# Second attention of a fused decoder: steps of two heads by one query block, spread inverse sums, output weight in the last pair

## The chip, the cores and the metric

One core of one Trainium2 chip runs the whole kernel. The metric is the device time in microseconds of one execution; lower is better. TensorE (PE) multiplies matrices into PSUM banks of 512 f32 columns, VectorE (DVE) and ScalarE (ACT) read PSUM, GpSimd (POOL) works on SBUF alone, and SyncE (SP) issues the transfers. Each engine takes its instructions in order and waits on semaphores.

## The reference

Two decoder layers on x of 2 x 512 tokens by 128: gated linear attention, cross attention, a mixture of experts; then a T5 attention, a bidirectional attention with a context and a quantized feed-forward layer. The change touches the T5 attention ("the second attention") alone. With 16 heads of 64 it computes, on normalised x:

```python
q, k, v = x @ wq, x @ wk, x @ wv                 # 128 -> 16 heads x 64, each
s = q @ k.T + bias[head, bucket(key - query)]    # no scale; bias from rel_bias
p = softmax(s)
x = x + concat_heads(p @ v) @ wo                 # 1024 -> 128
```

## The kernel before

A row is one head by one block of 128 queries: 16 heads x 2 batches x 4 blocks = 128 rows. Heads come in eight pairs (`PAIRS`); a pair has `ROWS` = 16 rows, two pairs make one turn of a loop (`BODY` = 32), and all engines run `t5_steps`: step s issues row s's scores and later stages of earlier rows (`on(s, lag, last)`), so that a row is drawn out over `LAG` = 8 steps. The order within a step is written out by hand on each engine.

Per row. TensorE: scores (L1220, f16 operands split in a high and a low part; the split halves of q lie one above the other in the 128 rows, 2 products of 512 columns) into bank 0 or 1; four transposes of the exponentials (L854) into bank 2 or 3; the context (L1231, 8 f16 products of 128 columns, probabilities split in two) into bank 4; the product with the head's rows of the output weight (L1211, f32, two passes) into bank 5. VectorE: scores plus bias strip, with the row minimum of the negated sum (L1707, `SN`, `nmx`); the reciprocal of the sum (L1690); the low part of the probabilities (L1720). ScalarE: exponential with row sum (L797); the high part of the probabilities (L810); eviction of the context (L791, `CTT`); eviction of the output product scaled by the inverse sum (L785, `OS`). POOL adds `OS` to X (L531), copies the bias strips and splits the qkv weights.

The projections of the next pair are 12 jobs (`t5_job`), one in each of 12 of the 16 steps: three or six products into bank 6 or 7 (L1184 for q and k, L1180 for v), the high part by ScalarE (`high_part`, L771, L769), the low part by VectorE (`low_part`, L1683). SyncE then lays the parts of q and k one above the other by eight transfers per pair (`stack_pair`, L356, L360), and loads the pair's rows of the output weight twice. For pair 0 these jobs and transfers come ahead of step 0.

After the last row, `norm_stats` and `norm_rows` of the first four tiles run inside the last steps (`NORM_STEP`), then the next attention begins (L1735).

## Time and profile before

| | us |
|---|---|
| median of 3 runs | 546.7 (546.38 to 551.78) |
| profiled execution | 549.21 |
| its span, first to last instruction | 547.4 |

The page gives busy time by engine. A timeline line gives the start and length of an instruction or of a few merged ones; engines start an instruction before the one ahead has left the pipe, so the distance from start to start is what one costs in a stream, and the length is what a waiter sees. The TensorE clock is given as a share of 2.4 GHz.

### The profile page before, as it was taken

What the parts mean: (1) busy time and instruction counts of PE and PEld (TensorE: products, weight loads), DVE (VectorE), ACT (ScalarE), POOL (GpSimd) and SP (SyncE); (2) the same over time, 40 slices, a digit from 0 to 9 for tenths busy, and PEclk for the clock granted to TensorE, in tenths of its full rate; (3) what the DMA queues carried; (4) which work ended last, traced back from release to release, by engine and by line L of the source; (5) the groups of instructions that cost most, each with busy time, mean ns of one, the idle gap of its engine ahead of it and who ended that gap; (6) DMA issues with size and microseconds to landing.
All of it is one profiled execution on the core that took longest, in us unless ns stands there. A gap on an engine that the chain in (4) does not pass through costs nothing.

```text
span 547.4 us, 12975 instructions
## 1 busy us (share of the span) xinstructions
PE 481.9 (88%) x4074; PEld 373.9 (68%) x4074; DVE 410.5 (75%) x1154; ACT 363.6 (66%) x996; POOL 159.6 (29%) x292
## 2 busy tenths in 40 slices
PE   4699858998786998549999989999999999989997
PEld 1245545777672776427888878887888888867866
DVE  3856858676776799738889878887898898754675
ACT  3834434444328587329999999998999999932140
POOL 4091352000013357201343324332433322230100
PEclk9989989999987899679999999999999999996899
DMA  7499553000000020061414140412423230000001
GB/s 235 65 102 104 65 176 123 1 1 1 2 0 10 30 72 25 1 131 38 95 39 104 27 106 11 97 43 50 91 49 77 49 79 1 2 2 1 0 1 40
DMA packets 23839, 29.32 MB, mean 54 GB/s; under 512 B 2262, under 2 KB 14848, under 8 KB 23789
## 3 DMA queue, kind: packets, MB, share of 16 engines
q1 hardware_dynamic: 23789, 28.73, 24.9%
q8 instruction: 22, 0.36, 0.3%
q14 instruction: 28, 0.23, 0.1%
HBM read 11.42 MB, written 4.72 MB: 29 GB/s over the span
## 4 chain that ended last, share of the span: by engine, by line
PE 52%; ACT 18%; DVE 16%; issue 9%; POOL 2%; DMA 1%; ACTq 0%; SPq 0%; POOLq 0%; DVEq 0%
PE bank L854 8%; ACT PT L810 8%; PE bank L1220 5%; PE bank L1231 5%; PE bank L1211 4%; PE bank L1078 4%; ACT PEX L797 4%; PE bank L1148 3%; PE bank L1135 3%; PE bank L859 2%; PE bank L1030 2%; ACT OS L785 2%; POOL X L531 2%; PE bank L1184 2%; DVE Y L1360 2%
## 5 line engine op out<-in xcount | busy, mean ns | idle before, releaser
L531 POOL TENSOR_TENSOR X<-X,OS 128x128 f32<-128x128 f32 x128 | 58.4, 456 | 179.9 <-ACT OS L785 179.9
L797 ACT ACTIVATE PEX<-SN,nmx 128x512 f32<-128x512 f32 x128 | 100.2, 782 | 9.4 <-DVE nmx L1707 9.4
L1707 DVE CUSTOM_DVE_ANT_0 SN<-bank,strip 128x512 f32<-128x512 f32 x128 | 86.4, 675 | 8.8 <-PE bank L1220 8.7
L1720 DVE TENSOR_TENSOR PT<-bank,PT 128x512 f16<-128x512 f32 x128 | 87.4, 683 | 1.5 <-ACT PT L810 1.3
L1231 PEld LDWEIGHTS bank<-PT,TV 128*128 128x128 f16 x1024 | 67.8, 98 | 29.0
L1220 PE MATMUL bank<-TK,TQ 128*128 128x512 f16 x256 | 77.3, 385 | 7.9 <-DMA TK<-RAWK 7.9
L810 ACT CAST PT<-bank 128x512 f16<-128x512 f32 x128 | 82.4, 643 | 0.3 <-PE bank L854 0.3
L1231 PE MATMUL bank<-PT,TV 128*128 128x128 f16 x1024 | 78.1, 219 | 0.0
L854 PE MATMUL bank<-cs,PEX 128*128 128x128 f32 x512 | 77.8, 275 | 0.2 <-DVE PT L1720 0.2
L785 ACT ACTIVATE OS<-bank,rps 128x128 f32<-128x128 f32 x128 | 56.0, 438 | 4.8 <-issue 3.6
L854 PEld LDWEIGHTS bank<-cs,PEX 128*128 128x128 f32 x512 | 57.0, 142 | 1.3 <-issue 0.4
L1211 PE MATMUL bank<-wos,CTT 128*128 128x128 f32 x256 | 53.2, 290 | 4.4 <-ACT OS L785 3.4
L1211 PEld LDWEIGHTS bank<-wos,CTT 128*128 128x128 f32 x256 | 38.4, 189 | 9.1 <-issue 3.3
L1690 DVE RECIPROCAL rps<-psm 128x1 f32<-128x1 f32 x128 | 20.9, 163 | 30.1 <-PE bank L1220 29.6
L791 ACT COPY CTT<-bank 128x128 f32<-128x128 f32 x128 | 41.0, 320 | 0.5 <-PE bank L1231 0.3
L1184 PE MATMUL bank<-YP,WP 128*128 128x256 f16 x192 | 33.1, 293 | 1.5 <-DVE YP L1671 1.4
L859 PE MATMUL bank<-ones 128*128 128x128 f32 x244 | 33.1, 292 | 0.0
L1220 PEld LDWEIGHTS bank<-TK,TQ 128*128 128x128 f16 x256 | 25.2, 99 | 11.0 <-issue 8.6
L859 PEld LDWEIGHTS bank<-ones 128*128 128x128 f32 x244 | 30.9, 205 | 1.6 <-issue 1.6
L797 ACT ACTIVATION_READ_ACCUMULATOR PEX<-SN,nmx 128x1 f32 x128 | 31.6, 247 | 0.0
L1613 DVE TENSOR_TENSOR HID<-PT,HID 128x512 f16<-128x512 f32 x32 | 25.8, 846 | 5.7 <-ACT HID L742 5.1
L1148 PE MATMUL bank<-w2p,HID 128*128 128x128 f16 x384 | 24.4, 227 | 6.2 <-DVEq L1636 3.7
(279 smaller groups left out, 912.9 us busy)
## 6 DMA issues: line engine op xcount, KB each, us to landing
TK<-RAWK SPq DMA_DIRECT2D x32, 256.0 KB, 4.4
bias_rows<-biasr SPq DMA_DIRECT2D x1, 4096.0 KB, 43.5
TQ<-RAWQ SPq DMA_DIRECT2D x32, 128.0 KB, 2.4
band<-bias_rows SPq DMA_DIRECT2D x1, 3072.0 KB, 11.5
wqkv<-in_twqkv SPq DMA_DIRECT2D x8, 192.0 KB, 3.9
w1s<-in_w SPq DMA_DIRECT2D x8, 128.0 KB, 2.1
w2s<-in_w SPq DMA_DIRECT2D x8, 128.0 KB, 2.1
wos<-in_two SPq DMA_DIRECT2D x16, 64.0 KB, 2.3
```

Source lines behind the costliest of these rows:

```text
L531: gp.tensor_tensor(x_tile, x_tile, OS[:, r % 2, :], ALU.add).then_inc(sm["to_ready"], 1)
L785: sc.activation(OS[:, r % 2, :], bank[5][:, 0:P], ACT.Copy, scale=rps[:, r % 8:r % 8 + 1]).then_inc(sm["os_ready"], 1)
L797: sc.activation(PE_[:, r % 2, :], SN[:, r % 2, :], ACT.Exp, bias=nmx[:, r % 2:r % 2 + 1], scale=-1.0, accum_out=psm[:, r % 8:r % 8 + 1]).t ...
L810: sc.copy(PT1[:, r % 4, :], bank[2 + r % 2][:, :]).then_inc(sm["pt1_ready"], 1)
L854: return nc.tensor.transpose(out_, in_, ident[0:n, 0:n])
L859: mm(bank[b][:, 2 * P:3 * P], ones[:, :], ones[:, :], start=True, stop=True)
L1184: ins = mm(o[:, 0:2 * P], WP[u][:, w_part, w:w + P], YP[:, x_part, 2 * P * g:2 * P * g + 2 * P], start=(k == 0), stop=(k == 2))
L1211: mm(bank[5][:, 0:P], CTT[:, r % 2, :], wos[u][:, h, :], start=True, stop=True).then_inc(sm["to_mm"], 1)
L1220: ins = mm(bank[s % 2][:, :], TQ[u][:, h, S * b + P * qt:S * b + P * qt + P], TK[u][:, part, h, S * b:S * b + S], start=(part == 0), stop= ...
L1231: ins = mm(bank[4][:, 0:P], TV[u][:, TG * b + kt, h, :, :].rearrange("p n d -> p (n d)"), pt[:, r % 4, P * kt:P * kt + P], start=(part == ...
L1707: vv.tensor_tensor_reduce(out=SN[:, r % 2, :], in0=bank[r % 2][:, :], in1=strip[u][:, h, c:c + S], scale=-1.0, scalar=3.0e38, op0=ALU.add, ...
L1720: vv.tensor_tensor(PT2[:, r % 4, :], bank[2 + r % 2][:, :], PT1[:, r % 4, :], ALU.subtract).then_inc(sm["pt2_ready"], 1)
```

## The change

A step is now two heads by one query block: 64 steps, `ROWS` = 8 and `BODY` = 16 for a turn of two pairs, lag 5. The heads of a pair sit in rows 0 to 63 and 64 to 127 of q and k as the projection leaves them: the stacking transfers and the raw copies are gone, and the scores are three products (high x high, high x low, low x high) of 64 rows for each head, alternating between the heads. Exponentials overwrite `SN`, a ring of four. The transposed probabilities are f32 (head 0 evicted by ScalarE, head 1 by VectorE), v stays f32, and the context of both heads goes to the two column halves of bank 6. The inverse sums are spread over 64 partitions per head by a product with the identity (columns 128 to 255 of bank 6), copied to `rpb` by ScalarE, and VectorE multiplies the context by them while it evicts it to `CTX`, which keeps all pairs. The product with the output weight (loaded once, whole, to `WO`) is issued in the last pair alone: in each of its eight steps seven products for one tile of X, and from step 13 to 20 of the last turn one more with the last pair's context; VectorE adds each result to X. Projections are six jobs of 512 columns, all through bank 7; the v jobs have no low part. Those of pair 0 use four banks, and its v jobs come behind the scores of step 0. The core of the diff:

```diff
 TH, TD = 16, 64
 PAIRS = TH // 2
-ROWS = 2 * NT
+ROWS = NT
 BODY = 2 * ROWS
-LAG = 8
-NORM_STEP = BODY + 3
-PROJECTIONS = [(kind, g) for kind in "qkv" for g in range(NT // 2)]
+LAG = 5
+RING = 4
+NORM_STEP = BODY + 2
+PROJECTIONS = [("q", 0), ("k", 0), ("q", 1), ("k", 1), ("v", 0), ("v", 1)]
 JOBS = len(PROJECTIONS)
-JOB_BANKS = (6, 7, 4, 5)
-JOBS_FROM = 2
-STACK = 8 * 16
+SPLIT_JOBS = 4
+JOB_BANK = 7
+FIRST_BANKS = (6, 7, 4, 5, 6, 7)
+JOBS_FROM = 1
...
-            RAWQ = t5("RAWQ", [P, 2, TOK], F16)
-            RAWK = t5("RAWK", [P, 2, TOK], F16)
             TQ = [t5(f"TQ{u}", [P, 2, TOK], F16) for u in range(2)]
-            TK = [t5(f"TK{u}", [P, 2, 2, TOK], F16) for u in range(2)]
-            TV = [t5(f"TV{u}", [P, NT, 2, 2, TD], F16) for u in range(2)]
-            SN = t5("SN", [P, 2, 512])
-            nmx = t5("nmx", [P, 2])
-            PE_ = t5("PEX", [P, 2, 512])
-            psm = t5("psm", [P, 8])
-            rps = t5("rps", [P, 8])
-            PT1 = t5("PT1", [P, 4, 512], F16)
-            PT2 = t5("PT2", [P, 4, 512], F16)
-            CTT = t5("CTT", [P, 2, P])
-            OS = t5("OS", [P, 2, P])
+            TK = [t5(f"TK{u}", [P, 2, TOK], F16) for u in range(2)]
+            TV = [t5(f"TV{u}", [P, NT, P]) for u in range(2)]
+            SN = t5("SN", [P, RING, 2, S])
+            nmx = t5("nmx", [P, RING, 2])
+            psm = t5("psm", [P, RING, 2])
+            rps = t5("rps", [P, RING, 2])
+            PTO = t5("PTO", [P, 2, S])
+            PTE = Z[:, :, :].rearrange("p (h t) c -> p h (t c)", h=2)
+            CTX = t5("CTX", [P, PAIRS, TOK])
+            rpb = YT[:, 0:P]
+            WO = XB
+            def probs_t(r, h):
+                return (PTE, PTO)[r % 2][:, h, :]
...
+            sp.wait_ge(sm["x_done"], 4)
+            sp.dma_start(WO[:, :, :], two.rearrange("(n p) c -> p n c", p=P)).then_inc(sm["ld_wo"], 16)
+            for pair in range(PAIRS):
+                if pair >= 2:
+                    sp.wait_ge(sm["tw_split"], (pair - 1) * 2)
+                pair_qkv(pair, pair % 2)
...
-                if on(s, LAG, last):
-
-                    r = s - LAG
-                    u, b, qt, h = where(r)
-                    pool.wait_ge(sm["os_ready"], n - 7)
-                    pool.wait_ge(sm["to_ready"], n - 6)
-                    x_tile = X[:, TG * b + qt, :]
-                    gp.tensor_tensor(x_tile, x_tile, OS[:, r % 2, :], ALU.add).then_inc(sm["to_ready"], 1)
...
+                if on(s, 1, last):
+                    r = s - 1
+                    for h in range(2):
+                        act.wait_ge(sm["ttr_ready"], (n - 1) * 2 + h + 1)
+                        p = SN[:, r % RING, h, :]
+                        sc.activation(p, p, ACT.Exp, bias=nmx[:, r % RING, h:h + 1], scale=-1.0,
+                                      accum_out=psm[:, r % RING, h:h + 1]).then_inc(sm["exp_ready"], 1)
+                if on(s, 4, last):
+                    act.wait_ge(sm["tpv_mm"], n - 3)
+                    if s >= 5:
+                        act.wait_ge(sm["ctt_ready"], n - 4)
+                    sc.copy(rpb[:, :], bank[6][:, P:2 * P]).then_inc(sm["rb_ready"], 1)
                 if on(s, 2, last):
-                    act.wait_ge(sm["ttr_ready"], n - 1)
                     r = s - 2
                     if s >= 4:
-                        act.wait_ge(sm["tt_mm"], n - 3)
-                    sc.activation(PE_[:, r % 2, :], SN[:, r % 2, :], ACT.Exp, bias=nmx[:, r % 2:r % 2 + 1], scale=-1.0,
-                                  accum_out=psm[:, r % 8:r % 8 + 1]).then_inc(sm["exp_ready"], 1)
-                job = t5_job(s - 1, last)
+                        act.wait_ge(sm["tpv_mm"], n - 3)
+                    act.wait_ge(sm["tt_mm"], (n - 2) * 2 + 1)
+                    sc.copy(probs_t(r, 0), bank[4][:, :]).then_inc(sm["pta_ready"], 1)
+                job = t5_job(s, last)
                 if job:
                     j, u, ahead = job
-                    if j == 0:
-
-                        act.wait_ge(sm[f"stack{1 - u}"], (i + ahead + u) * STACK)
-                    high_part(((i + ahead) * 2 + u) * JOBS, j, u)
-                if on(s, 3, last):
-
-                    r = s - 3
-                    act.wait_ge(sm["tt_mm"], n - 2)
-                    sc.copy(PT1[:, r % 4, :], bank[2 + r % 2][:, :]).then_inc(sm["pt1_ready"], 1)
-                if last and s == NORM_STEP + 2:
+                    high_part(i * 2 + ahead, j, u)
+                if last and s == NORM_STEP + 1:
...
+            def out_tile(tile, pairs, done):
+                pe.wait_ge(sm["ctt_ready"], pairs[-1] * ROWS + tile + 1)
+                pe.wait_ge(sm["to_ready"], done)
+                for p in pairs:
+                    ins = mm(bank[JOB_BANK][:, 0:P], CTX[:, p, P * tile:P * tile + P], WO[:, p, :], start=(p == pairs[0]), stop=(p == pairs[-1]))
+                ins.then_inc(sm["wo_mm"], 1)
             pe.wait_ge(sm["tw_split"], 2)
-            for j in range(JOBS):
-                if j >= 4:
-                    pe.wait_ge(sm["pj_ready"], j - 3)
-                project(0, j, 0, 4)
-            pe.wait_ge(sm["pj_ready"], JOBS)
+            for j in range(SPLIT_JOBS):
...
+                    u, b, qt = where(s)
+                    if qt == 0:
+                        pe.wait_ge(sm["pj_ready"], (i * 2 + s // ROWS) * SPLIT_JOBS + 2 * b + 2)
                     if s >= 2:
-                        pe.wait_ge(sm["ttr_ready"], n - 1)
-                    for part in range(2):
-                        ins = mm(bank[s % 2][:, :], TQ[u][:, h, S * b + P * qt:S * b + P * qt + P],
-                                 TK[u][:, part, h, S * b:S * b + S], start=(part == 0), stop=(part == 1))
-                    ins.then_inc(sm["ts_mm"], 1)
-                if on(s, 5, last):
-                    r = s - 5
-                    u, b, qt, h = where(r)
-                    if s >= 6:
-                        pe.wait_ge(sm["ctt_ready"], n - 5)
-                    for part, (pt, ready) in enumerate(((PT1, "pt1_ready"), (PT2, "pt2_ready"))):
-                        pe.wait_ge(sm[ready], n - 4)
-                        for kt in range(TG):
-                            ins = mm(bank[4][:, 0:P], TV[u][:, TG * b + kt, h, :, :].rearrange("p n d -> p (n d)"),
-                                     pt[:, r % 4, P * kt:P * kt + P], start=(part == 0 and kt == 0), stop=(part == 1 and kt == TG - 1))
-                    ins.then_inc(sm["tpv_mm"], 1)
+                        pe.wait_ge(sm["ttr_ready"], (n - 1) * 2)
+                    pe.wait_ge(sm["ln_yt"], 10)
+                    for k, (q_part, k_part) in enumerate(PRODUCTS):
+                        for h in range(2):
+                            r = slice(TD * h, TD * h + TD)
+                            ins = mm(bank[2 * (s % 2) + h][:, :], TQ[u][r, q_part, S * b + P * qt:S * b + P * qt + P],
+                                     TK[u][r, k_part, S * b:S * b + S], start=(k == 0), stop=(k == 2))
+                            if k == 2:
+                                ins.then_inc(sm["ts_mm"], 1)
+                    if s == 0:
+                        for j in range(SPLIT_JOBS, JOBS):
+                            pe.wait_ge(sm["pj_ready"], j - SPLIT_JOBS + 1)
+                            project(j, 0, FIRST_BANKS[j])
...
+                if on(s, 2, last):
+                    r = s - 2
+                    if s == 2:
+                        pe.wait_ge(sm["pj_ready"], SPLIT_JOBS)
+                    for h in range(2):
+                        pe.wait_ge(sm["exp_ready"], (n - 2) * 2 + h + 1)
+                        if s >= 3:
+                            pe.wait_ge(sm[("pta_ready", "ptb_ready")[h]], n - 2)
+                        for kt in range(TG):
+                            ins = tr(bank[4 + h][:, P * kt:P * kt + P], SN[:, r % RING, h, P * kt:P * kt + P])
+                        ins.then_inc(sm["tt_mm"], 1)
+                if on(s, 3, last):
+                    r = s - 3
+                    u, b, qt = where(r)
+                    if qt == 0:
+                        pe.wait_ge(sm["pj_hi"], (i * 2 + r // ROWS) * JOBS + SPLIT_JOBS + b + 1)
+                    if s >= 4:
+                        pe.wait_ge(sm["ctt_ready"], n - 3)
+                    pe.wait_ge(sm["rps_ready"], n - 2)
+                    for h in range(2):
+                        mm(bank[6][TD * h:TD * h + TD, P:2 * P], rps[:, r % RING, h:h + 1].to_broadcast([P, TD]), ident, start=True, stop=True)
+                    pe.wait_ge(sm["pta_ready"], n - 2)
+                    pe.wait_ge(sm["ptb_ready"], n - 2)
+                    for kt in range(TG):
+                        for h in range(2):
+                            d = slice(TD * h, TD * h + TD)
+                            ins = mm(bank[6][d, 0:P], TV[u][:, TG * b + kt, d], probs_t(r, h)[:, P * kt:P * kt + P],
+                                     start=(kt == 0), stop=(kt == TG - 1))
+                    ins.then_inc(sm["tpv_mm"], 1)
+                for done, tile, pairs in out_tiles(s, last):
+                    if done == 0:
+                        pe.wait_ge(sm["ld_wo"], 16)
+                        pe.wait_ge(sm["pj_hi"], PAIRS * JOBS)
+                    out_tile(tile, pairs, done)
...
+                    if (s - 1) % ROWS == 0:
+                        dve.wait_ge(sm["strip_ready"], (i * 2 + (s - 1) // ROWS + 1) * 6)
+                    if s >= 5:
+                        dve.wait_ge(sm["tt_mm"], (n - 4) * 2)
+                    dve.wait_ge(sm["ts_mm"], n * 2)
+                    dve.sem_inc(sm["ttr_turn"], 1)
+                for h in range(2):
+                    if on(s, 1, last):
+                        r = s - 1
+                        u, b, qt = where(r)
+                        c = P * (TG - 1 - qt)
+                        vv.tensor_tensor_reduce(out=SN[:, r % RING, h, :], in0=bank[2 * (r % 2) + h][:, :], in1=strip[u][:, h, c:c + S], scale=-1.0,
+                                                scalar=3.0e38, op0=ALU.add, op1=ALU.min,
+                                                accum_out=nmx[:, r % RING, h:h + 1]).then_inc(sm["ttr_ready"], 1)
+                    if h == 0 and on(s, 2, last):
+                        r = s - 2
+                        dve.wait_ge(sm["exp_ready"], (n - 1) * 2)
+                        vv.reciprocal(rps[:, r % RING, :], psm[:, r % RING, :]).then_inc(sm["rps_ready"], 1)
+                if on(s, 4, last):
+                    r = s - 4
+                    u, b, qt = where(r)
+                    dve.wait_ge(sm["rb_ready"], n - 3)
+                    c = P * (TG * b + qt)
+                    dst = CTX[:, bass.ds(i * 2 + r // ROWS, 1), c:c + P].rearrange("p o c -> p (o c)")
+                    vv.tensor_tensor(dst, bank[6][:, 0:P], rpb[:, :], ALU.mult).then_inc(sm["ctt_ready"], 1)
+                if on(s, 2, last):
+                    r = s - 2
+                    if s >= 4:
+                        dve.wait_ge(sm["tpv_mm"], n - 3)
+                    dve.wait_ge(sm["tt_mm"], (n - 1) * 2)
+                    vv.tensor_copy(probs_t(r, 1), bank[5][:, :]).then_inc(sm["ptb_ready"], 1)
+                job = t5_job(s, last)
                 if job:
                     j, u, ahead = job
-                    low_part(((i + ahead) * 2 + u) * JOBS, j, u)
-                if on(s, 4, last):
-
-                    r = s - 4
-                    if s >= 8:
-                        dve.wait_ge(sm["tpv_mm"], n - 7)
-                    dve.wait_ge(sm["pt1_ready"], n - 3)
-                    vv.tensor_tensor(PT2[:, r % 4, :], bank[2 + r % 2][:, :], PT1[:, r % 4, :], ALU.subtract).then_inc(sm["pt2_ready"], 1)
+                    if j < SPLIT_JOBS:
+                        low_part(i * 2 + ahead, j, u)
+                for done, tile, pairs in out_tiles(s, last):
+                    dve.wait_ge(sm["wo_mm"], done + 1)
+                    dve.wait_ge(sm["to_ready"], done)
+                    vv.tensor_tensor(X[:, tile, :], bank[JOB_BANK][:, 0:P], X[:, tile, :], ALU.add).then_inc(sm["to_ready"], 1)
 
                 if last and s == NORM_STEP:
-                    dve.wait_ge(sm["to_ready"], n - NORM_STEP + BODY - ROWS // 2 + 2)
+                    dve.wait_ge(sm["to_ready"], 12)
                     norm_stats(6, 0, X)
-                if last and s == NORM_STEP + 3:
+                if last and s == NORM_STEP + 2:
...
+    j, ahead = s % ROWS - JOBS_FROM, s // ROWS + 1
+    if 0 <= j < JOBS and not (last and ahead > 1):
+        return j, ahead % 2, ahead
     return None
+def out_tiles(s, last):
+    order = [(s_, tile, pairs) for s_ in range(ROWS, BODY + LAG)
+             for tile, pairs in ((s_ - ROWS, range(PAIRS - 1)), (s_ - ROWS - LAG, range(PAIRS - 1, PAIRS))) if 0 <= tile < NT]
+    return [(done, tile, pairs) for done, (s_, tile, pairs) in enumerate(order) if s_ == s and last]
```

## Rows read from the trace of the kernel before

**Rows 1.** The page, part 1: busy time, share of the span and instructions by engine.
```profile
PE 481.9 (88%) x4074; PEld 373.9 (68%) x4074; DVE 410.5 (75%) x1154; ACT 363.6 (66%) x996; POOL 159.6 (29%) x292
```
**Rows 2.** Stretches: busy us (x instructions) by engine, TensorE clock, DMA share, GB/s.
```profile
421.00:450.00 29.00, 28.98 (x306) 24.49 (x304) 25.89 (x76) 29.00 (x93) 9.55 (x22) 1.00 0.27 60
450.00:484.00 34.00, 32.62 (x322) 26.46 (x321) 26.82 (x83) 32.12 (x100) 10.54 (x24) 1.00 0.01 2
```
**Rows 3.** Timeline, TensorE, start of the second attention: start, us, instructions, idle before.
```profile
229.07 5.25 PE L1184 MATMUL bank<-YP,WP 128*128 128x256 f16 x24 [1.40 <-DVE YP L1671]
...
243.62 1.86 PE L1220 MATMUL bank<-TK,TQ 128*128 128x512 f16 x4 [7.87 <-DMA TK<-RAWK]
```
**Rows 4.** Timeline, all engines, end of the second attention.
```profile
482.03 1.35 DVE L1360 TENSOR_SCALAR Y<-X,mv,rstd 128x128 f32<-128x128 f32 x4 [1.21 <-ACT rstd L577]
...
483.34 0.46 POOL L531 TENSOR_TENSOR X<-X,OS 128x128 f32<-128x128 f32 x1 [0.55 <-ACT OS L785]
```
**Rows 5.** Timeline, TensorE, one row with a projection.
```profile
311.76 0.49 PE L1184 MATMUL bank<-YP,WP 128*128 128x256 f16 x3
312.09 0.60 PE L854 MATMUL bank<-cs,PEX 128*128 128x128 f32 x4
312.52 0.39 PE L1211 MATMUL bank<-wos,CTT 128*128 128x128 f32 x2
312.75 0.59 PE L1220 MATMUL bank<-TK,TQ 128*128 128x512 f16 x2
313.18 0.61 PE L1231 MATMUL bank<-PT,TV 128*128 128x128 f16 x8
313.63 0.49 PE L1184 MATMUL bank<-YP,WP 128*128 128x256 f16 x3
```
**Rows 6.** Timeline, ScalarE, one row without a projection.
```profile
450.72 0.73 ACT L797 ACTIVATE PEX<-SN,nmx 128x512 f32<-128x512 f32 x1
...
451.44 0.57 ACT L810 CAST PT<-bank 128x512 f16<-128x512 f32 x1
451.90 0.38 ACT L785 ACTIVATE OS<-bank,rps 128x128 f32<-128x128 f32 x1
452.19 0.27 ACT L791 COPY CTT<-bank 128x128 f32<-128x128 f32 x1
452.35 0.72 ACT L797 ACTIVATE PEX<-SN,nmx 128x512 f32<-128x512 f32 x1
```
**Rows 7.** Timeline, VectorE.
```profile
249.56 0.68 DVE L1720 TENSOR_TENSOR PT<-bank,PT 128x512 f16<-128x512 f32 x1
...
250.23 0.67 DVE L1707 CUSTOM_DVE_ANT_0 SN<-bank,strip 128x512 f32<-128x512 f32 x1
250.83 0.08 DVE L1707 DVE_READ_ACCUMULATOR2_ANT nmx<- 128x1 f32 x1
```
**Rows 8.** Timelines of the GLA stage (the first up to 38.30): rows*columns of a product.
```profile
38.15 0.44 PE L922 MATMUL bank<-QX,KC 128*64 128x256 f32 x2
...
38.73 1.10 PE L949 MATMUL bank<-V,AM 128*128 128x64 f32 x8
...
40.35 0.70 PE L938 MATMUL bank<-V,KPT 64*128 64x256 f32 x4
...
40.98 0.70 PE L963 MATMUL bank<-wA,YT 128*128 128x512 f32 x1
```
**Rows 9.** Group of one line: shapes, count, busy us, mean ns, idle before.
```profile
L1492 DVE TENSOR_TENSOR CX<-bank,rc 128x128 f32<-128x128 f32 x8 | 2.3, 291 | 0.5 <-DVE rc L1489 0.2
```
**Rows 10.** Timeline, first row: VectorE's minimum pass, ScalarE's exponential.
```profile
244.79 0.69 DVE L1707 CUSTOM_DVE_ANT_0 SN<-bank,strip 128x512 f32<-128x512 f32 x1 [8.18 <-PE bank L1220]
...
245.53 0.72 ACT L797 ACTIVATE PEX<-SN,nmx 128x512 f32<-128x512 f32 x1 [9.37 <-DVE nmx L1707]
```
**Rows 11.** Timeline, TensorE, at a turn of the loop.
```profile
316.15 0.49 PE L1211 MATMUL bank<-wos,CTT 128*128 128x128 f32 x2 [1.60 <-ACT OS L785]
```
**Rows 12.** Timeline, POOL: one part of a weight split.
```profile
331.48 0.92 POOL L516 TENSOR_TENSOR WP<-wqkv,WP 128x384 f16<-128x384 f32 x1
```

158 lines of the change are left out of this document (34 added, 124 removed).

## The prediction

> **What bounds the kernel now.** I read the page first: TensorE is the busiest engine [rows 1]. The busy time of stretches comes next: between 421 and 450 us TensorE and ScalarE are both busy for practically the whole stretch, at full clock, and VectorE for nine tenths [rows 2]. That is the second attention, the only stage touched. It starts with the first score product at 243.62 us and ends with the last POOL addition, at 483.80 [rows 3, 4]: 240.2 us for 128 rows (one head, one query block), about 1.88 us each.
>
> Three timelines of single rows say why no engine alone can be relieved. On TensorE, start to start, a row costs 0.33 (projection), 0.43 (four transposes), 0.23 (output product, f32, two passes of about 0.11), 0.43 (two 512-column f16 score products of 0.216) and 0.45 us (eight context products of 0.056): 1.87, with no gap [rows 5]. On ScalarE a row without a projection costs 0.72 (exponential with its sum), 0.46 (512-column eviction), 0.29 and 0.16 (the two 128-column evictions): 1.63 [rows 6], and 0.25 more with one. On VectorE it is 0.60 for the minimum pass, 0.67 for the 512-column subtraction with the reciprocal [rows 7]. So TensorE and ScalarE tie at 1.87 in a row with a projection, and ScalarE sets 1.62 without one. One head pair (12 rows with, 4 without) takes about 12 x 1.87 + 4 x 1.62 = 28.9 us.
>
> **The change, per step (two heads, one query block).** TensorE:
> - Scores: six products of 64 rows instead of four of 128. The heads lie in different row halves. Do halves run side by side? The GLA stage has such pairs. Two column halves at line 922 had both started within 0.15 us, and four passes of 256 columns were over 0.58 us after the first; row halves at line 938 took 0.63 [rows 8]. One after another, four such passes would be 4 x 0.22 = 0.88 by the 0.11 of a 128-column pass. So they run in pairs. Scores: 3 x 0.216 = 0.65 (serial: 1.30).
> - Transposes stay: 8 x 0.11 = 0.87.
> - Context in f32, column halves: 16 passes in pairs, 8 x 0.11 = 0.87 (serial 1.75). The spread of inverse sums: 2 x 0.11 = 0.22 more.
> - Projection: the same columns in half as many jobs, 0.65 each, in six of eight steps.
> - Output product: two of 0.23 fewer per step, but see the last pair.
> - Form changes. 0.58 and 0.63 us against 2 x 0.213 leave 0.15 and 0.20 us per group for entering and leaving a tiled form [rows 8]. There are three changes of form per step (row halves, full, column halves): 0.2 + 0.2 + 0.15 = 0.55. I take the whole; zero is the low end, since before has them at 0 in this stage.
>
> TensorE sum: 0.65 + 0.87 + 0.87 + 0.22 + 0.55 = 3.17, with a projection 3.82, against 3.74 and 3.24 for two rows before. The Trainium skill (TensorEngine Tiling (Array Packing), Key Properties) says that changing the tiling mode drains the engine. The trace agrees: line 949 starts 0.58 us behind the start of the group before it, where the streaming alone explains 0.43. By the rule the sum is the one above; without it, it would be 0.55 lower.
>
> ScalarE: 2 x 0.72, one copy of spread sums 0.15 to 0.29, one probability eviction 0.46, a 512-column projection eviction 0.46: 2.65 at most. VectorE: 2 x 0.60, reciprocal and eviction 0.67 together, product at context eviction about 0.2 (length 0.29 for such a shape [rows 9]), low part 0.60: 2.7. Both are relieved, from 3.74. If sums of work decided, TensorE would set the pace.
>
> **But the order of waits decides.** Row s-3's context product may not start before VectorE has evicted row s-4 from bank 6. That eviction waits for the ScalarE copy of spread sums, which is queued behind both exponentials of row s-1; these wait for the minimum passes of the same step. From the start of the first minimum pass: 0.74 to the first exponential (244.79 to 245.53, [rows 10]), +0.72 second exponential at 1.46, +0.72 copy at 2.18, ready at 2.50 (0.32; the like eviction has a length of 0.27 [rows 6], and I add 0.05 for the handover), VectorE product 2.52 to 2.81, TensorE starts at 2.85.
>
> Loop A, in steps with a q or k projection: behind the copy (2.18) ScalarE evicts the probabilities (+0.16), then the projection (+0.46), which takes 0.60 till VectorE can begin the low part (the like cast has a length of 0.57 [rows 6]), which holds VectorE for 0.60, before the next step's minimum pass: 2.18 + 0.16 + 0.46 + 0.60 + 0.60 = 4.0, with waits between 4.05. A v projection has no low part now, so TensorE's own 3.82 decides. With none: 2.81 less the overlap = 2.78, +0.60 for the VectorE eviction = 3.4. A pair: 4 x 4.05 + 2 x 3.82 + 2 x 3.4 = 30.6 us, against 28.9. So the middle loses 1.7 us per pair although every engine but TensorE has less to do.
>
> **The last pair.** Each of steps 56 to 63 issues seven f32 output products, 14 passes x 0.11 = 1.54 us. Total output work falls (64 instead of 128 products), but where it sits matters: VectorE's addition from bank 7 is the last thing in its step, and its next minimum pass is queued behind it. The loop is 2.85 (to the context product) + 0.15 + 0.22 + 0.87 (spread and context) + 0.2 (change of form) + 1.54 + 0.3 (end of product to VectorE) = 6.1, +0.2 for the addition's issue distance: about 6.2 us per step. Steps 61 to 63 have a second product and addition, serial through the same bank: +0.75. Last pair: 5 x 6.2 + 3 x 6.95 = 51.9 us, where before spent 16 x 1.62 = 25.9. POOL's additions, hidden before (they run 0.46 us after the row's last eviction, and nobody waits for them but POOL [rows 4]), move into this loop. The product of the first step also waits for the output weight and the last projection, both long done. The drain: step 64 has the loop to the context and one short product, 2.85 + 1.24 + 0.8 = 4.9; the two last contexts go copy, VectorE product, spread, context, output product, addition one after another, 0.3 + 0.3 + 1.24 + 0.8 = 2.6 each; two short products 0.8 each; and on VectorE's queue the normalised rows of four tiles, 1.35 [rows 4], and their statistics, put at 0.9: about 14.
>
> **The start.** The eight stacking DMAs per pair and SyncE's waits for them vanish; only the first is exposed, as TensorE's 7.87 us wait [rows 3]. Now four 512-column projections (half the clock there: 24 products of 256 columns took 5.25 us, so 12 of 512 take about 5.1) end at 234.2, the score product follows, the two v projections after it, and their ScalarE evictions (queued ahead of the first exponential) let that begin at 237.4. The first step counts from 236.6. SyncE now loads the whole output weight once, long before, and eight qkv weights; POOL's weight splits (0.92 us for one part [rows 12]) and strip copies (now two in a step) stay off the path: each has two or more steps of slack, no other engine's queue stands behind them but the jobs and minimum passes of the next pairs, and POOL's 128 additions are gone. If that cover went, a split of 1.8 us would show per pair.
>
> **Sum.** Step 1 at 236.6; 55 steps: 7 x 30.6 - 3.4 = 210.8; -1.5 for unfilled first steps; +3.4 for loop turns (one cost TensorE 1.60 us [rows 11], another about as much, the same loop count remains); start of the last pair 449.3; +51.9 = 501.2; +14 = 515.2. Before: 483.8. Difference +31.4. The profiled execution took 549.2 us (span 547.4), so about 580.6; the median of the three runs is 546.7, 2.5 lower: **578 us**.
>
> **Rivals.**
> - R1, only TensorE's work counts (queues run ahead, waits hide): a pair is 6 x 3.82 + 2 x 3.17 = 29.3, a last-pair step 3.17 + 1.54 = 4.7. Ends at 236.6 + 201.9 - 1.5 + 3.4 + 37.7 + 10 = 488, +4: 551; within 1%. For it: ring buffers of four; against: bank 6 and bank 7 are single. Chance 0.08. A mixture, loop A real but last pair shorter (5 us a step), gives 568 and belongs to the forecast.
> - R2, the other side: changes of form cost nothing when products queue up, and the copy is never late. The pace is then 3.17 - 0.55 = 2.62, and 3.27 with a projection, 24.9 a pair, 4.2 a last-pair step: 236.6 + 171.7 - 1.5 + 3.4 + 33.6 + 10 = 454, so 517, faster. It decides once form changes and waits together cost under 0.5 us per step. For it: all three engines' sums are below before's. Against: [rows 8] and loop A, made of instructions each priced. Chance 0.12.
> - R3, halves don't overlap at N = 128 and here (serial): +0.65 + 0.87 + 0.22 = 1.74 per step: 4.9 and 5.55 a step, 43.2 a pair, last-pair steps 7.3: 578 + 7 x 12.6 + 9 = about 675. Against: [rows 8]. Chance 0.05. Partly (weight loads not hidden in a half, +0.4 a step): about 600, in the range.
> - R4, the clock falls: TensorE is busy 4.7 of 6.2 us in the last pair. Before, the clock stays at 2.4 GHz between 450 and 484 [rows 2] with less work at the end. Chance 0.03, +15 us.
>
> **Numbers.** Forecast 0.72, R1 0.08, R2 0.12, R3 0.05, R4 0.03. About 1% is what a measurement can tell from no change. Faster by over 1%: 0.12 (R2). Within 1%: 0.08. Slower: 0.80. Unknown terms: forms 0.55 down to 0.3 (only v and empty steps move, -5 us), copy and handover latencies 0.1 a step (7 us), last pair 5.3 to 7 us a step (-7, +6), unhidden weight loads (+20). With R1 inside, the range is 550 to 602; the forecast's own part of it is 560 to 602.
>
> **What would show it.** Loads at the score product: alternate heads start a few ns apart. Minimum passes two by two, with pairs of steps 4.0 to 4.1 us apart in four of eight, 3.8 in two, 3.4 in two; TensorE idle ahead of the spread product, released by VectorE's context eviction; steps of about 6.2 us in the last eight, the minimum pass waiting behind the addition; the first score product near 234.4; last addition near 514. Wrong if steps of the middle come under 3.6 us on average, or the last pair under 40 us.

## The result, and the profile after

The changed kernel took 581.2 us (median of 4 runs, 579.2 to 584.3), the kernel before 549.2 us beside it (median of 4, 546.4 to 557.6): 1.060 times as long, with a 95% interval from 1.051 to 1.070. (Ratios, here and below, are of fast executions alone; one that took over 1.5% more than the fastest of its kernel, such as the one of 557.6, is left out.) The forecast was 578, in a range from 550 to 602. The profiled execution took 581.8 us with a span of 580.0, against a span of 547.4 before.

The page and its groups of instructions (columns: count, busy us, mean ns, idle before and what ended it), after:

```profile
PE 490.6 (85%) x4234; PEld 351.0 (61%) x4234; DVE 368.7 (64%) x1042; ACT 291.6 (50%) x692; POOL 103.9 (18%) x164
...
L738 ACT ACTIVATE SN<-SN,nmx 128x512 f32<-128x512 f32 x128 | 91.4, 714 | 99.0 <-DVE nmx L1664 99.0
...
L1677 DVE TENSOR_TENSOR CTX<-bank,YT 128x128 f32 (+1 forms) x64 | 18.6, 291 | 70.6 <-ACT YT L744 70.6
```

ScalarE idles 99.0 us ahead of its exponentials, always for VectorE's minimum, and VectorE idles 70.6 us ahead of the context eviction, always for ScalarE's copy of the spread sums (YT is the memory in which that copy lies). The engines now wait for one another in a ring. The windows of [rows 2] have changed in the same way; the middle of the stage and the last pair, after:

```profile
421.00:448.40 27.40, 25.46 (x282) 17.76 (x284) 18.48 (x54) 18.19 (x48) 0.91 (x3) 1.00 0.00 1
454.56:496.00 41.44, 31.48 (x306) 24.14 (x300) 17.00 (x57) 14.81 (x42) 0.00 (x0) 1.00 0.00 1
```

The columns after the length are PE, PEld, DVE, ACT and POOL with their instructions, then the granted clock. Before, TensorE and ScalarE filled their stretch. Now ScalarE is busy for two thirds of the first one and for a third of the second, and even TensorE leaves 10 of 41 us free in the last pair. The clock is full in both, so it explains nothing here.

**A step of the middle** (q or k projection), first minimum pass at 302.80, next one at 306.80. VectorE:

```profile
302.80 0.68 DVE L1664 CUSTOM_DVE_ANT_0 SN<-bank,strip 128x512 f32<-128x512 f32 x1
...
305.34 0.29 DVE L1677 TENSOR_TENSOR CTX<-bank,YT 128x128 f32 x1 [1.18 <-ACT YT L744]
305.55 0.68 DVE L1683 COPY Z<-bank 128x512 f32<-128x512 f32 x1
306.19 0.69 DVE L1646 TENSOR_TENSOR TK<-bank,TK 128x512 f16<-128x512 f32 x1
306.80 0.68 DVE L1664 CUSTOM_DVE_ANT_0 SN<-bank,strip 128x512 f32<-128x512 f32 x1
```

ScalarE and TensorE in the same step:

```profile
303.52 0.72 ACT L738 ACTIVATE SN<-SN,nmx 128x512 f32<-128x512 f32 x1 [1.36 <-DVE nmx L1664]
304.24 0.71 ACT L738 ACTIVATE SN<-SN,nmx 128x512 f32<-128x512 f32 x1
304.95 0.24 ACT L744 COPY YT<-bank 128x128 f32<-128x128 f32 x1
305.10 0.58 ACT L750 COPY Z<-bank 128x512 f32<-128x512 f32 x1
305.57 0.59 ACT L726 CAST TK<-bank 128x512 f16<-128x512 f32 x1
```
```profile
303.36 0.82 PE L1128 MATMUL bank<-YP,WP 128*128 128x512 f16 x3
304.02 1.04 PE L798 MATMUL bank<-cs,SN 128*128 128x128 f32 x8
305.69 0.44 PE L1196 MATMUL bank<-cs,rps 128*64 128x128 f32 x4 [0.63 <-DVE CTX L1677]
305.95 1.04 PE L1202 MATMUL bank<-PTO,TV 128*64 128x128 f32 x16
306.93 0.39 PE L1155 MATMUL bank<-TK,TQ 64*128 64x512 f16 x2
```

Read as a loop: minimum 302.80, first exponential 303.52, second 304.24, copy 304.95, probabilities 305.10, cast 305.57, low part 306.19, next minimum 306.80. That is 4.00 us, and TensorE stands idle for 0.63 of them, released by the context eviction.

**A step of the last pair**, first minimum pass at 454.56, next one at 460.65:

```profile
454.56 0.69 DVE L1664 CUSTOM_DVE_ANT_0 SN<-bank,strip 128x512 f32<-128x512 f32 x1
...
456.71 0.24 ACT L744 COPY YT<-bank 128x128 f32<-128x128 f32 x1
...
456.99 0.29 DVE L1677 TENSOR_TENSOR CTX<-bank,YT 128x128 f32<-128x128 f32 x1 [1.06 <-ACT YT L744]
...
457.34 0.44 PE L1196 MATMUL bank<-cs,rps 128*64 128x128 f32 x4 [1.30 <-DVE CTX L1677]
457.61 1.04 PE L1202 MATMUL bank<-Z,TV 128*64 128x128 f32 x16
458.58 1.83 PE L1136 MATMUL bank<-XB,CTX 128*128 128x128 f32 x14
460.34 0.82 PE L1155 MATMUL bank<-TK,TQ 64*128 64x512 f16 x6
460.44 0.29 DVE L1692 TENSOR_TENSOR X<-bank,X 128x128 f32<-128x128 f32 x1 [2.56 <-PE bank L1136]
460.65 0.68 DVE L1664 CUSTOM_DVE_ANT_0 SN<-bank,strip 128x512 f32<-128x512 f32 x1
```

VectorE waits 2.56 us for the fourteen output passes, and the next minimum pass is queued behind the addition. (XB is the memory in which the whole output weight lies.)

The start and the end of the stage, after (compare [rows 3] and [rows 4]):

```profile
231.54 4.95 PE L1128 MATMUL bank<-YP,WP 128*128 128x512 f16 x12 [1.40 <-DVE YP L1639]
...
236.43 0.82 PE L1155 MATMUL bank<-TK,TQ 64*128 64x512 f16 x6
...
237.76 0.68 DVE L1664 CUSTOM_DVE_ANT_0 SN<-bank,strip 128x512 f32<-128x512 f32 x1
```
```profile
512.33 0.29 DVE L1692 TENSOR_TENSOR X<-bank,X 128x128 f32<-128x128 f32 x1 [0.64 <-PE bank L1136]
512.53 3.04 DVE L1328 TENSOR_SCALAR Y<-X,mv,rstd 128x128 f32<-128x128 f32 x4
515.50 0.54 DVE L1707 TENSOR_SCALAR RH<-wB,colp 128x77 f32<-128x77 f32 x2
```

**Where the 32.6 us went** (580.0 less 547.4). From the first projection to the end of the stage it was 254.7 us before (229.07 to 483.80) and is 284.0 now (231.54 to 515.50): +29.2. The stages ahead, with the same code, ran 2.5 us later in this execution; what follows took 64.5 instead of 63.6. Within the 29.2, cut at the minimum passes of the same rows in both traces: the start gave 9.5 back (from the first projection to the first minimum pass 6.2 instead of 15.7, most of it the score product, 4.89 behind the first projection instead of 14.55). The middle cost 8.6 more (210.7 against 202.1), the last pair 25.9 more (52.0 against 26.1), and the drain behind it 4.2 more (15.1 against 10.9).

The middle lost less than the 7 x 1.7 of the prediction, for two reasons. A pair without a turn of the loop had taken 29.1 us in the trace before and not 28.9, so that the loss per pair is 1.5. And the two turns of the loop had cost 2.1 and 1.7 us before (pairs of 31.2 and 30.8), and cost 0.5 and 0.2 after. The unfilled first steps took a part of this back: they shorten the first pair by 0.8 us, and did by 2.1 before.

### The profile page after: what moved, and what is told of

Its sections match the earlier page's. It is cut to its first block, busy times and chain, and to the rows that moved or that the text cites. A ratio compares the mean times of both kernels' runs of the same rounds, so it can differ in the third digit from the quotient of the medians.

```text
span 580.0 us, 12093 instructions
## 1 busy us (share of the span) xinstructions
PE 490.6 (85%) x4234; PEld 351.0 (61%) x4234; DVE 368.7 (64%) x1042; ACT 291.6 (50%) x692; POOL 103.9 (18%) x164
## 4 chain that ended last, share of the span: by engine, by line
PE 46%; DVE 24%; issue 14%; ACT 13%; DVEq 1%; DMA 1%; ACTq 0%; SPq 0%
ACT SN L738 7%; PE bank L798 5%; DVE SN L1664 5%; PE bank L1202 4%; PE bank L1022 3%; PE bank L1092 3%; PE bank L1136 3%; PE bank L803 3%; PE bank L1079 2%; PE bank L1155 2%; PE bank L974 2%; DVE Y L1328 2%; PE bank L1196 2%; PE bank L1128 2%; DVE stats L1318 1%
## 5 line engine op out<-in xcount | busy, mean ns | idle before, releaser
L738 ACT ACTIVATE SN<-SN,nmx 128x512 f32<-128x512 f32 x128 | 91.4, 714 | 99.0 <-DVE nmx L1664 99.0
L798 PE MATMUL bank<-cs,SN 128*128 128x128 f32 x512 | 67.6, 275 | 0.0
L798 PEld LDWEIGHTS bank<-cs,SN 128*128 128x128 f32 x512 | 57.1, 141 | 14.1 <-issue 5.9
L1677 DVE TENSOR_TENSOR CTX<-bank,YT 128x128 f32 (+1 forms) x64 | 18.6, 291 | 70.6 <-ACT YT L744 70.6
L1155 PE MATMUL bank<-TK,TQ 64*128 64x512 f16 x384 | 52.6, 380 | 0.0
L1196 PE MATMUL bank<-cs,rps 128*64 128x128 f32 x256 | 28.1, 296 | 28.7 <-DVE CTX L1677 19.2
L1202 PE MATMUL bank<-Z,TV 128*64 128x128 f32 x512 | 33.8, 273 | 0.0
L803 PEld LDWEIGHTS bank<-ones 128*128 128x128 f32 x244 | 32.6, 215 | 1.6 <-issue 1.6
L1202 PE MATMUL bank<-PTO,TV 128*64 128x128 f32 x512 | 33.4, 273 | 0.0
L1128 PE MATMUL bank<-YP,WP 128*128 128x512 f16 x96 | 27.9, 410 | 3.9 <-DVE YP L1639 1.4
L1202 PEld LDWEIGHTS bank<-Z,TV 128*64 128x64 f32 x512 | 29.5, 137 | 0.0
L1202 PEld LDWEIGHTS bank<-PTO,TV 128*64 128x64 f32 x512 | 29.1, 137 | 0.0
```

The source lines that it names most:

```text
L738: sc.activation(p, p, ACT.Exp, bias=nmx[:, r % RING, h:h + 1], scale=-1.0, accum_out=psm[:, r % RING, h:h + 1]).then_inc(sm["exp_ready"], 1)
L798: return nc.tensor.transpose(out_, in_, ident[0:n, 0:n])
L803: mm(bank[b][:, 2 * P:3 * P], ones[:, :], ones[:, :], start=True, stop=True)
L1128: ins = mm(o[:, :], WP[u][:, w_part, w:w + P], YP[:, x_part, S * g:S * g + S], start=(k == 0), stop=(k == 2))
L1155: ins = mm(bank[2 * (s % 2) + h][:, :], TQ[u][r, q_part, S * b + P * qt:S * b + P * qt + P], TK[u][r, k_part, S * b:S * b + S], start=(k = ...
L1196: mm(bank[6][TD * h:TD * h + TD, P:2 * P], rps[:, r % RING, h:h + 1].to_broadcast([P, TD]), ident, start=True, stop=True)
```

## The experiments

For each kernel the stage is cut at the first minimum pass (T1), at step 56 with which the last pair begins (T56), at step 64 (T64), and where VectorE is through (End, the first write of RH). All are us of the profiled execution; "rest" is what follows End. The kernel before is cut at the same heads and query blocks, its rows 110 and 126, and its last POOL addition ends 0.16 us ahead of its End.

| kernel | T1 | T1 to T56 | T56 to T64 | T64 to End | rest | span |
|---|---|---|---|---|---|---|
| before | 244.8 | 202.1 | 26.1 | 11.0 | 63.4 | 547.4 |
| after | 237.8 | 210.7 | 52.0 | 15.1 | 64.5 | 580.0 |
| e1_add_later | 240.8 | 210.6 | 38.9 | 13.2 | 63.3 | 566.8 |
| e2_sums_between | 236.2 | 199.4 | 46.6 | 14.3 | 62.0 | 558.5 |
| e3_low_later | 236.7 | 195.0 | 52.0 | 16.6 | 61.8 | 562.0 |
| e4_every_step | 235.8 | 222.5 | 29.1 | 15.1 | 60.5 | 563.0 |
| e5_all | 237.0 | 191.0 | 37.1 | 15.4 | 64.4 | 544.9 |
| e6_full_width | 240.8 | 249.1 | 59.9 | 19.4 | 61.8 | 631.0 |
| e7_fourth_form | 235.2 | 202.2 | 52.0 | 16.6 | 62.9 | 568.9 |
| e8_no_spread | 240.8 | 179.7 | 35.4 | 13.8 | 62.1 | 531.8 |

And the distances from one step's first minimum pass to the next, as read from the traces: a pair of the middle that holds no turn of the loop, then the last pair. In a pair the first four steps have q and k projections, the fifth and sixth v, the last two none. In e3, e5, e7 and e8 the projection stands behind the transposes and so comes into the distance after its own step's.

```
after  4.55 4.00 4.00 4.00 3.35 3.98 3.35 3.39 | 6.14 6.10 6.08 6.13 6.08 7.02 7.39 7.08
e1     as after                                | 3.39 4.94 4.77 4.78 4.78 4.78 5.71 5.71
e2     4.27 4.00 4.00 4.01 2.64 3.97 3.02 3.02 | 5.60 5.39 5.39 5.43 5.38 6.32 6.68 6.38
e3     3.35 3.66 3.67 3.67 3.67 3.69 3.69 3.34 | as after
e4     4.70 4.04 4.50 4.04 3.87 4.07 3.44 3.84 | 3.84 3.44 3.84 3.44 ...
e5     3.01 3.67 3.67 3.67 3.67 3.69 3.69 3.02 | 3.02 4.78 4.78 4.77 4.78 5.00 5.00 5.00
e6     5.38 4.73 4.73 4.73 4.10 4.76 4.13 4.13 | ...  7.01 7.00 7.04 7.00 7.94 8.30 7.99
e7     3.49 3.81 3.82 3.82 3.82 3.84 3.84 3.34 | as after
e8     2.79 3.45 3.45 3.45 3.45 3.47 3.47 2.80 | ...  4.56 4.56 4.56 4.56 4.78 4.78 4.78
```

**1. VectorE adds the output product one step later.** Nothing but the place of the addition in VectorE's order changes.

```diff
+                for done, tile, pairs in out_tiles(s - 1, last):
+                    dve.wait_ge(sm["wo_mm"], done + 1)
+                    dve.wait_ge(sm["to_ready"], done)
+                    vv.tensor_tensor(X[:, tile, :], bank[JOB_BANK][:, 0:P], X[:, tile, :], ALU.add).then_inc(sm["to_ready"], 1)
                 if on(s, 4, last):
...
-                for done, tile, pairs in out_tiles(s, last):
-                    dve.wait_ge(sm["wo_mm"], done + 1)
-                    dve.wait_ge(sm["to_ready"], done)
-                    vv.tensor_tensor(X[:, tile, :], bank[JOB_BANK][:, 0:P], X[:, tile, :], ALU.add).then_inc(sm["to_ready"], 1)
```

> The changed kernel, but VectorE adds an output product to X one step later, behind the second minimum pass of the next step instead of ahead of its first. Nothing is left out. Theory W (the order of waits decides): the steps of the last pair, 6.1 us each in the changed kernel, fall to TensorE's own work, 0.27 (spread) + 0.97 (context) + 1.76 (output) + 0.75 (scores) + 0.97 (transposes) = 4.7; steps 61 to 63 from 7.1 to about 5.7; last pair 52 to about 41 us, total about 570. Rival P (TensorE's work decides everywhere): no instruction of TensorE changes, so the last pair stays at 52 and the total at 581.

Measured: 562.5 us (560.7 to 568.6), 1.026 times the kernel before (1.022 to 1.029). TensorE in the last pair of this kernel:

```profile
460.15 1.83 PE L1136 MATMUL bank<-XB,CTX 128*128 128x128 f32 x14
461.91 0.82 PE L1155 MATMUL bank<-TK,TQ 64*128 64x512 f16 x6
462.66 1.09 PE L798 MATMUL bank<-cs,SN 128*128 128x128 f32 x8
463.68 0.44 PE L1196 MATMUL bank<-cs,rps 128*64 128x128 f32 x4
```

TensorE does the same work as in the changed kernel, and a step falls from 6.1 to 4.78 us: it has no idle time left ahead of the spread product (1.30 us before the edit). So 13.2 us of the last pair's 52.0 were the wait for the addition, and not TensorE's work; rival P, by which only TensorE's work counts, had them stay. The other 12.8 over before (38.9 less 26.1) are work: the steps now come at TensorE's own pace. The middle did not move (210.6), as it should not. The stage is 15.0 us shorter, where about 11 were expected. (The execution profiled here, 568.6, was the longest of the five; its first minimum pass came 3.0 us later than in the changed kernel.)

**2. The copy of the spread sums between the two exponentials.**

```diff
-                if on(s, 1, last):
-                    r = s - 1
-                    for h in range(2):
+                for h in range(2):
+                    if on(s, 1, last):
+                        r = s - 1
...
-                if on(s, 4, last):
-                    act.wait_ge(sm["tpv_mm"], n - 3)
...
-                    sc.copy(rpb[:, :], bank[6][:, P:2 * P]).then_inc(sm["rb_ready"], 1)
+                    if h == 0 and on(s, 4, last):
+                        act.wait_ge(sm["tpv_mm"], n - 3)
...
+                        sc.copy(rpb[:, :], bank[6][:, P:2 * P]).then_inc(sm["rb_ready"], 1)
```

> The changed kernel, but ScalarE copies the spread sums between the two exponentials instead of behind both; nothing else moves, nothing is left out. W: context eviction and next context product come 0.7 us earlier in a step. Steps with a q or k projection stay at 4.0 (loop A holds both exponentials and the copy in either order), empty steps fall from 3.35 to about 3.0, the last pair's steps from 6.1 to 5.4: 7 x 0.7 + 8 x 0.7, total about 571. P: 581.

Measured: 559.3 us (559.0 to 560.3), ratio 1.021 (1.018 to 1.024). ScalarE in the last pair:

```profile
447.34 0.72 ACT L738 ACTIVATE SN<-SN,nmx 128x512 f32<-128x512 f32 x1 [3.24 <-DVE nmx L1664]
448.06 0.24 ACT L744 COPY YT<-bank 128x128 f32<-128x128 f32 x1
448.21 0.72 ACT L738 ACTIVATE SN<-SN,nmx 128x512 f32<-128x512 f32 x1
```

The copy starts 0.72 earlier behind the first exponential, and a step of the last pair is 0.7 shorter (6.1 to 5.39). In the middle the q and k steps keep their 4.00 us, although the context eviction is 0.7 earlier: their loop goes through the second exponential, the projection's cast and the low part, where the copy's place does not matter. The other steps lose what their loop had: 2.64 and 3.97 with v, 3.02 without. A pair takes 28.9 instead of 30.6. The kernel gained more than was expected (559.3, for 571). Of the 21.5 us between the two spans, 17.4 lie in the stage (11.2 in the middle, where 4.9 were expected, 5.5 in the last pair, 0.7 behind it); 4.1 lie in the stages ahead and behind, which have the same code.

**3. The low part one step later, and the projection behind the transposes.** Both orders have to move together, since the low part frees bank 7 for the next job.

```diff
+                if on(s, 2, last):
+                    r = s - 2
...
+                            ins = tr(bank[4 + h][:, P * kt:P * kt + P], SN[:, r % RING, h, P * kt:P * kt + P])
+                        ins.then_inc(sm["tt_mm"], 1)
                 job = t5_job(s, last)
...
-                            ins = tr(bank[4 + h][:, P * kt:P * kt + P], SN[:, r % RING, h, P * kt:P * kt + P])
-                        ins.then_inc(sm["tt_mm"], 1)
...
+                job = t5_job(s - 1, last)
+                if job:
+                    j, u, ahead = job
+                    if j < SPLIT_JOBS:
+                        low_part(i * 2 + ahead, j, u)
                 if on(s, 4, last):
...
-                job = t5_job(s, last)
```

> The changed kernel, but VectorE makes the low part of a projection one step later, behind the second minimum pass, and TensorE issues the projection behind the transposes, so that bank 7 is free in time. Nothing is left out. W: loop A is broken, the steps with a q or k projection fall from 4.0 (the first of a pair 4.55) to TensorE's own 3.62; a pair from 30.6 to 28.6, the last pair stays at 52: total about 567. P: 581.

Measured: 563.2 us (562.4 to 565.0), ratio 1.028 (1.025 to 1.032). VectorE of the middle:

```profile
327.71 0.67 DVE L1664 CUSTOM_DVE_ANT_0 SN<-bank,strip 128x512 f32<-128x512 f32 x1
328.30 0.68 DVE L1646 TENSOR_TENSOR TK<-bank,TK 128x512 f16<-128x512 f32 x1
329.57 0.29 DVE L1682 TENSOR_TENSOR CTX<-bank,YT 128x128 f32 x1 [0.58 <-ACT YT L744]
```

The low part fills the time in which VectorE had waited for the copy, and the six distances with a projection are now 3.66 to 3.69 us, at which TensorE has no idle time. So the four steps of 4.00 were the loop through the low part. From T1 to T56 it is 15.7 us less, 4.0 of them in the first pair (25.9 instead of 29.9) and 1.9 in each later one (28.7 instead of 30.6, as expected); the last pair did not move. Of the 18.0 us between the two spans 3.8 lie in the stages ahead and behind, which have the same code; that is what brings the total to 563.2, for 567 expected.

**4. The output product in every step.** The part of the change that puts all output work in the last pair is undone: each step adds its own product from free columns of bank 6.

```diff
-                for done, tile, pairs in out_tiles(s, last):
...
-                    out_tile(tile, pairs, done)
...
+                    mm(bank[6][:, 2 * P:3 * P], CTX[:, u, c:c + P], WOP[:, u, :], start=True, stop=True).then_inc(sm["wo_mm"], 1)
```

> The changed kernel with one part undone: the output product is issued in every step, one f32 product for both heads behind the context product, into bank 6, columns 256 to 383, and VectorE adds it to X in the next step behind the context eviction; POOL copies the pair's output weight to a fixed place. The number of products (64) is the same. W: seven pairs cost 0.1 to 1 us more each (+0.33 us of TensorE per step, partly in its idle time), the last pair falls from 52 to about 27 us and the drain by 3: total about 558. P: the same products and one more change of form per step, so 581 or up to 6 slower.

Measured: 565.5 us (564.8 to 567.9), ratio 1.034 (1.030 to 1.038). TensorE in every second step:

```profile
336.54 0.49 PE L1232 MATMUL bank<-WOP,CTX 128*128 128x128 f32 x2
...
339.79 0.44 PE L1212 MATMUL bank<-cs,rps 128*64 128x128 f32 x4 [0.39 <-DVE X L1706]
```

The last pair fell from 52.0 to 29.1, close to the 27 that were expected, but a pair of the middle takes 32.5, above the 31.6 that I had put as its upper end: the addition now stands ahead of the spread product, which waits 0.39 us for it. Over the whole stage it gains 11.0 us (22.9 in the last pair less 11.9 in the middle), less than e1 does by moving one wait in the last pair (15.0), and the total is 565.5, for 558 expected. In the order of the changed kernel a product in each step thus brings an addition into each step's loop. No run spreads the products over the steps in the better order of e5, below. An estimate from distances: one product a step adds 0.42 us to TensorE (336.54 to 336.96), 27 over 64 steps, where e5's collected products take 8 x 1.76 + 8 x 0.22 = 16. By this estimate collecting them is no loss by itself.

**5. All together.** Edits 1 to 3, and in the last pair the pair's own product goes to free columns of bank 6 while bank 7 sums the other seven, one step earlier.

```diff
-                for done, tile, pairs in out_tiles(s, last):
...
+                if last and 12 <= s < 20:
...
+                    mm(bank[6][:, 2 * P:3 * P], CTX[:, PAIRS - 1, P * tile:P * tile + P], WO[:, PAIRS - 1, :], start=True, stop=True).then_inc(sm["wob_mm"], 1)
+                if last and 8 <= s < 16:
...
-                    out_tile(tile, pairs, done)
...
+                    for p in range(PAIRS - 1):
+                        ins = mm(bank[JOB_BANK][:, 0:P], CTX[:, p, P * tile:P * tile + P], WO[:, p, :], start=(p == 0), stop=(p == PAIRS - 2))
```

> The three edits of e1, e2 and e3 together: low part one step later, spread sums copied between the exponentials, additions to X behind the second minimum pass of the next step; and the last pair's own output product goes to bank 6, columns 256 to 383, one step earlier, so that it does not wait for bank 7. Nothing is left out. W: a pair is 6 x 3.67 + 2 x 3.0 = 28.0 us, the last pair's steps 4.8 to 4.9, the drain 2 shorter: 580 - 7 x 2.6 - 14 - 2 = about 546, level with the kernel before (547.6). If the three gains share one wait they don't add: 555 or more.

Measured: 543.1 us (median of 12 runs, 541.5 to 550.2), the kernel before beside it 547.7: ratio 0.992 (0.989 to 0.995); 546 were expected. It is the fastest that does all of the work. Its window of the middle:

```profile
421.00:448.00 27.00, 27.00 (x292) 20.89 (x290) 15.47 (x52) 15.97 (x43) 0.00 (x0) 1.00 0.01 1
```

TensorE is busy for 27.00 of 27.00 us, with the other two engines at less than 60%. No loop of waits is left in the middle, so a step here is TensorE's own work: 3.67 with a projection, 3.02 without, 4.78 with seven output products.

**6. The context products at full width.** Both heads are multiplied with all 128 columns of v and summed, so the context is not the reference's; nothing runs in column halves but the spread.

```diff
-                            d = slice(TD * h, TD * h + TD)
-                            ins = mm(bank[6][d, 0:P], TV[u][:, TG * b + kt, d], probs_t(r, h)[:, P * kt:P * kt + P],
-                                     start=(kt == 0), stop=(kt == TG - 1))
+                            ins = mm(bank[6][:, 0:P], TV[u][:, TG * b + kt, :], probs_t(r, h)[:, P * kt:P * kt + P],
+                                     start=(kt == 0 and h == 0), stop=(kt == TG - 1 and h == 1))
```

> The changed kernel, but each context product takes v of both heads as weights (128 columns) and writes all 128 rows of bank 6, so that no two run in column halves; both heads' products are summed into one, so the context's numbers are not the attention's. It shows what the halves are worth. If they run in pairs (forecast): the context goes from 0.97 to about 1.75 + 0.1 us, TensorE's step from 3.62 to 4.5 with a projection and from 2.97 to 3.85 without, a pair from 30.6 to 34.7, total about 617. R3 (halves run one after another anyway): no change, 581.

Measured in a single execution: 632.8 us. TensorE:

```profile
301.58 0.44 PE L1196 MATMUL bank<-cs,rps 128*64 128x128 f32 x4
301.94 2.05 PE L1201 MATMUL bank<-PTO,TV 128*128 128x128 f32 x16
303.93 0.82 PE L1155 MATMUL bank<-TK,TQ 64*128 64x512 f16 x6
```

The sixteen passes last 1.99 us start to start, where they took 0.98 in halves (305.95 to 306.93): the halves do run in pairs, and that is worth 1.0 us a step. The time came out 16 above what was expected, since more was lost than the passes: 1.01 for these and another 0.10 from the spread to the context (0.36 instead of 0.26) make TensorE's own step 4.73, which passes the loop of 4.00 and sets the pace in every step. Everything one after another (R3) would have shown no difference at all between the two kernels here.

**7. One more change of form.** The edit is to e3's kernel: head 0's transposes stand ahead of the scores: four changes of form in a step instead of three, and the same work.

```diff
+                if on(s, 2, last):
+                    r = s - 2
...
+                    for kt in range(TG):
+                        ins = tr(bank[4][:, P * kt:P * kt + P], SN[:, r % RING, 0, P * kt:P * kt + P])
+                    ins.then_inc(sm["tt_mm"], 1)
...
-                    for h in range(2):
+                    for h in range(1, 2):
```

> e3 (where TensorE sets the step with a projection) with head 0's transposes issued ahead of the scores instead of behind them: the same instructions, but four changes of form per step instead of three. Nothing is left out. By the prediction's price (0.15 to 0.20 per form) the steps go from 3.67 to 3.85; by the distances in the changed kernel's own trace (0.05 to 0.11 per change) to 3.77; if a change of form is free, 3.67.

Measured in a single execution: 570.7 us. TensorE:

```profile
300.22 0.66 PE L798 MATMUL bank<-cs,SN 128*128 128x128 f32 x4
300.81 0.82 PE L1165 MATMUL bank<-TK,TQ 64*128 64x512 f16 x6
301.56 0.66 PE L798 MATMUL bank<-cs,SN 128*128 128x128 f32 x4
```

The steps with a projection take 3.82 instead of 3.67, between the 3.77 and the 3.85 of the expectation: one more group entered and left costs 0.15 us. Four transposes take 0.59 ahead of the scores, where four passes of 0.11 explain 0.44. So form changes have a price, and with TensorE as the bound a step pays it in full.

**8. Without the spread products.** The edit is to e5's kernel: it runs without the two spread products and their copy, so that the context is multiplied with whatever the memory of the copy holds; all other work is done.

```diff
-                        sc.copy(rpb[:, :], bank[6][:, P:2 * P]).then_inc(sm["rb_ready"], 1)
...
-                    for h in range(2):
-                        mm(bank[6][TD * h:TD * h + TD, P:2 * P], rps[:, r % RING, h:h + 1].to_broadcast([P, TD]), ident, start=True, stop=True)
```

> e5 without the spread of the inverse sums: the two products per step (four passes) and ScalarE's copy are left out, and VectorE multiplies the context by stale values, so the attention's context is not normalised. It prices the spread where TensorE sets the step. W: each step loses the distance from spread to context, 0.27 us: 3.67 to 3.40, 3.02 to 2.75, last pair's steps 4.78 to 4.5; 64 x 0.27 = 17, total about 526. Rival (the context product's start was held by the eviction anyway, and TensorE's spread fills a wait): 543.

Measured: 532.6 us (2 runs, 531.6 and 533.6), 0.971 of before (0.956 to 0.987); 526 were expected. The steps fall from 3.67 to 3.45, 3.02 to 2.80 and 4.78 to 4.56, 0.22 each time, which is the four passes, run two by two at 0.11, and nothing more, where the whole distance of 0.27 was expected; the change of form is paid by the context products anyway. The stage is 14.7 us shorter than in e5, of which 64 x 0.22 = 14.1. The sums spread by a product are thus the price of scaling at the eviction, and they use up more than e5 gains over before.

## Why the prediction was right

- **The bound of the middle.** "The order of waits decides" is what the changed trace shows, and e3 and e2 show it by taking it away: with the same TensorE work, T1 to T56 falls by 15.7 and by 11.2 us. Loop A was forecast at 4.05 (4.00 and 0.05 for waits) and is 4.00, and its single terms are 0.72, 0.72, 0.71, 0.15, 0.47, 0.62, 0.61 against 0.74, 0.72, 0.72, 0.16, 0.46, 0.60, 0.60. The durations of [rows 6], [rows 7] and [rows 10] carried over to the new order within 0.02.
- **A pair at 30.6.** Measured 30.6 in the profile, but its parts differ in three places that cancel. A v step was put at 3.82; the two take 3.35 and 3.98, 0.3 less together. The first q step takes 4.55 and not 4.05, because TensorE arrives at its transposes a projection later than in the steps without one, and ScalarE then waits 0.45 for them; the trace shows this wait, no experiment isolates it, and e3, which moves the projection behind them, has no such step. The other three q and k steps together are 0.15 less than forecast.
- **From T1 to T56.** Forecast 212.7, measured 210.7. The 3.4 for turns of the loop was the wrong term: the steps at the first are 4.24 and 4.19 instead of 4.00, the one at the second 4.15, and the two pairs are 0.5 and 0.2 longer, 0.7 in all. The 1.5 taken off for the unfilled first steps was too much and hides a part of it: the first pair took 29.9, 0.8 less than the others. A likely reason for the short turns, which no run isolates, is ScalarE: in [rows 11] TensorE's 1.60 were released by ScalarE, which was busy without a gap before [rows 2] and now idles in every step. TensorE's own idle time isn't needed for it: in e5 it is busy throughout and a pair with a turn takes no longer.
- **The changes of form** were the term with the wrong size. I took 0.55 a step from [rows 8]. In the changed trace the context to the scores takes 0.98 where 8 x 0.109 explain 0.87, the scores to the next group 0.76 for 0.65, the transposes to the spread 0.97 for 0.87, and the spread to the context 0.27 for 0.22: 0.10, 0.11, 0.10 and 0.05, so 0.36. TensorE's steps are 3.67 and 3.02 in e5, where the forecast had 3.82 and 3.17. It moved little here only because TensorE was not the bound in most steps. e7 prices one more group with a form of its own at 0.15. The Trainium skill (TensorEngine Tiling (Array Packing), Key Properties) says that a change of the tiling mode drains the engine, without a price; the measured 0.05 to 0.11 per change, and e7's 0.15, agree with it.
- **Halves in pairs.** Right: in the changed trace the two passes of a pair start 6 or 7 ns apart in the context and 3 or 4 ns apart in the scores, one pair of the context takes 0.109 us, and e6 loses 1.0 us a step without them. R3 (everything one after another) falls.
- **The last pair.** Forecast 51.9, measured 52.0: steps 6.08 to 6.14 (forecast 6.2) and, where two products are added, 7.02, 7.39 and 7.08 (6.95), so that two small errors cancel. Its mechanism, the next minimum pass behind the addition, is shown by e1: without that one place in the order a step takes 4.78 (R1 had 4.7).
- **The start.** The first score product came 4.89 us behind the first projection (forecast 5.1), without the wait for stacking DMAs. The first minimum pass was at 237.8 instead of 236.6, because the stages ahead ran 2.5 us later and the rest 1.3 us faster than I had it. The first exponential waited until 239.21 (forecast 237.4) behind the evictions of v. The next steps came 4.09 and 3.84 later, so little of that was passed on.
- **The drain.** Forecast 14, measured 15.1. I took the four normalised rows at 1.35 from [rows 4]; they took 3.04, beside POOL's additions:

```profile
512.76 2.48 POOL L508 TENSOR_TENSOR XB<-X,rowp 128x512 f32<-128x512 f32 x2 [90.85 <-DVEq L1702]
```

In the kernel before the same POOL instructions stood beside the two writes of RH, which took 2.52 us there and 0.54 here. In e1, whose only edit is a place in the order, the four rows end before POOL begins, and again the writes of RH stand beside it:

```profile
502.00 1.10 DVE L1328 TENSOR_SCALAR Y<-X,mv,rstd 128x128 f32<-128x128 f32 x4
503.44 2.49 POOL L508 TENSOR_TENSOR XB<-X,rowp 128x512 f32<-128x512 f32 x2 [78.59 <-DVEq L1705]
503.46 2.53 DVE L1710 TENSOR_SCALAR RH<-wB,colp 128x77 f32<-128x77 f32 x2
```

The slow-down thus changes its victim with the order: what stands beside the two POOL instructions takes 2 us longer, whichever it is. The Trainium skill (SBUF — State Buffer, SBUF: two separate sides) tells of a pair of ports that VectorE and GpSimd hold one at a time; the lengths agree with that, but no run here takes the POOL instructions away.
- **The rivals.** R1 (only TensorE's work) needed all waits to be hidden; e5 takes them away and lands at 543 us, below R1's 551, since the form changes cost less than R1 had. R2 (faster, at 517) needed 3.27 and 2.62 a step: e5 has 3.67 and 3.02 with TensorE busy throughout, so changes of form and the engine's work exclude it, whatever the waits do. R4: the granted clock is 1.00 in both windows.
- **The offset.** The end of the stage was forecast at 515.2 and came at 515.5. That is closer than the terms deserve, and luck in part: +1.2 at T1, -2.0 to T56, +0.1 in the last pair, +1.1 in the drain. Of the 3 us between 578 and 581.2, 2.5 are what was taken off because the execution profiled before was 2.5 above its median; the changed kernel's profiled execution was only 0.6 above its own.

Why e5 gains only 0.8% although the start alone gives 9.5 us back: its middle takes 191.0 us against 202.1 before, 11 less, because a pair now takes 28.1 instead of 29.1 and the turns of the loop show nothing. But the last pair takes 37.1 instead of 26.1, 11 more, because seven products of each tile wait for it, and the drain 4.5 more. From the first minimum pass to the end of the stage e5 takes 243.5 us (237.0 to 480.5), the kernel before 239.0 (244.79 to 483.80). What is gained is the start, less the drain.

## What to carry to other kernels

When a change lets work be done by fewer or wider instructions, write the new order of every queue out as loops (from one instruction to its own next turn), with single durations from the old trace; here these loops gave 30.6 us for a pair and 51.9 for the last one (measured 30.6 and 52.0), where sums of engine work gave 29.3 and 37.7. Then look in each loop for an instruction that is late and is queued ahead of one that others need at once: moving the addition, the copy, the low part with its projection, and one output product brought 35 us in the profile, 34 of them in this stage, without taking away any work. Work that is collected for the end is paid in its own time (12.8 us over before in e1's last pair), and a second time in waiting (13.2 us there) if the start of the next step is queued behind it.

## What the runs showed of the hardware

- **Stages with the same code vary more than expected.** The first minimum pass, ahead of which all nine kernels from the change on run the same code but for the last few microseconds, came between 235.2 us (e7) and 240.8 (e1, e6, e8). The granted clock over the first 225 us tells them apart: 0.91 in those three, 0.93 to 0.95 in the other six. Columns as in the windows above; e1, then e2 (first minimum pass at 236.2):

```profile
0.00:225.00 225.00, 186.81 (x1247) 130.10 (x1248) 156.07 (x403) 110.88 (x225) 69.94 (x110) 0.91 0.31 63
```
```profile
0.00:225.00 225.00, 181.07 (x1272) 125.25 (x1272) 160.96 (x428) 111.77 (x228) 72.69 (x112) 0.95 0.32 64
```

  So two spans can differ by 5 us without any cause in the changed stage. Parts of the stage are compared here from T1 on for that reason.
- **The first pass in a new form costs more**, and by how much depends on the form. The first full-width f32 pass of the context in e6, behind the spread's column halves, has 0.21 us to itself instead of 0.11, and the distance from the spread to the context is 0.36 instead of 0.26. The first transpose behind the context in e7 has 0.17, and the first pair of column halves behind the transposes in the changed kernel 0.16.
- **A turn of the loop can be nearly free**: 0.5 and 0.2 us in the changed kernel and nothing in e5 (pairs of 28.1 with and without one), against 2.1 and 1.7 in the kernel before.
